# Spreading one number per token over the partitions: three bf16 parts on diagonals instead of fp32 products with the identity

## What is computed

```python
x = x + attention_windowed(_layernorm(x))     # 16 heads of 8, window +-16, token 0 global
x = x + ffn_ternary(_layernorm(x))
x = x + rglru(_layernorm(x))                  # gated linear recurrence, both directions
x = x + ffn_ternary(_layernorm(x))
x = x + attention_full_1(_layernorm(x))       # 16 heads of 8, softmax over 1024 tokens
x = x + moe(_layernorm(x))                    # top 1 of 8 experts, one shared We, capacity n // 8
x = x + attention_full_2(_layernorm(x))
x = x + moe(_layernorm(x))
```

```python
def _layernorm(x, axis=-1, eps=1e-05):
    m = jnp.mean(x, axis=axis, keepdims=True)
    v = jnp.var(x, axis=axis, keepdims=True)
    return (x - m) / jnp.sqrt(v + eps)
...
router_logits = h @ Wg
probs = jax.nn.softmax(router_logits, axis=1)
best = jnp.argmax(probs, axis=1)
mask = jax.nn.one_hot(best, E, dtype=probs.dtype)
gate = jnp.sum(probs * mask, axis=1)
...
out = combine.reshape(n, E * cap) @ expert_out     # = gate * (h @ We + be) for tokens within capacity
```

## Time and profile before

| | |
|---|---|
| median of 3 runs | 1068.19 us |
| lowest, highest | 1066.82, 1069.66 us |
| the profiled execution, its own time | 1069.15 us |
| its span in the profile | 1067.4 us |
| first full attention's loop starts at about | 345 us |
| last slot ends, run 4 alone from about | 1041 us |
| TensorE, VectorE, ScalarE, GpSimd busy | 91%, 78%, 68%, 16% |

### The profile page before, as it was taken

How to read it: one execution, slowest core, us unless ns; L and a number is a source line. 1 busy time by engine, 2 the same in 40 slices (tenths; PEclk the granted TensorE clock), 3 DMA queues, 4 the chain that set the end, 5 groups by cost and what they waited for, 6 DMA issues and landing times.

```text
span 1067.4 us, 32392 instructions
## 1 busy us (share of the span) xinstructions
PE 973.9 (91%) x13373; PEld 442.7 (41%) x13373; DVE 835.3 (78%) x1035; ACT 726.8 (68%) x1469; POOL 165.6 (16%) x438
## 2 busy tenths in 40 slices
PE   6799999779786999999999999999999999999997
PEld 2445545433342234344444444444434444433443
DVE  4545745164854999999999899999989998998923
ACT  3613544348332499999777789977779986797880
POOL 8200101016300000000011220011231001100100
PEclk8789989879877999999999999999999999999999
DMA  3763432200008213220000015410003530010000
GB/s 108 199 196 87 108 88 76 63 1 1 1 11 261 61 48 76 63 46 19 27 14 15 13 55 151 93 27 13 13 24 108 122 73 13 13 39 27 13 28 24
DMA packets 60386, 64.47 MB, mean 60 GB/s; under 512 B 17424, under 2 KB 39184, under 8 KB 60112
## 3 DMA queue, kind: packets, MB, share of 16 engines
q1 hardware_dynamic: 60240, 62.40, 22.0%
HBM read 27.06 MB, written 35.32 MB: 58 GB/s over the span
## 4 chain that ended last, share of the span: by engine, by line
DVE 56%; PE 32%; issue 5%; DMA 3%; ACT 3%; SPq 1%; POOLq 0%; POOL 0%; DVEq 0%; ACTq 0%
DVE nmf L1676 47%; PE wide L692 22%; PE bank L692 10%; DVE xcsq L1447 1%; DVE xp L1447 1%; DMA x<-xT 1%; ACT scr L1206 1%; DVE xcsq L1456 1%; SPq L447 1%; DMA KQs<-mw_dram 1%; DVE res L1447 1%; ACT L1206 1%; DVE nmt L1615 1%; DVE big L1830 1%; DVE big L1447 0%
## 5 line engine op out<-in xcount | busy, mean ns | idle before, releaser
L1676 DVE TENSOR_REDUCE nmf<-wide 128x1 f32<-128x1024 f32 x512 | 589.4, 1207 | 16.4 <-PE wide L692 15.6
L1206 ACT ACTIVATE big<-wide 128x512 f32<-128x512 f32 x683 | 391.3, 601 | 82.5 <-PE wide L692 70.9
L692 PE MATMUL wide<-big,KQs 48*128 48x512 bf16 (+1 forms) x1376 | 348.9, 343 | 3.8 <-DVE nmf L1676 2.1
L692 PE MATMUL bank<-big,V 128*9 128x128 f32 x8192 | 320.2, 274 | 11.9
L692 PEld LDWEIGHTS bank<-big,V 128*9 128x9 f32 x8192 | 177.3, 90 | 232.3 <-ACT big L1206 194.8
L692 PE MATMUL wide<-KQs,big 50*128 50x512 bf16 (+1 forms) x1035 | 266.4, 323 | 0.0
L1206 ACT ACTIVATE big<-bank 128x512 f32<-128x512 f32 (+1 forms) x469 | 231.6, 514 | 39.5 <-PE bank L692 33.7
L692 PE MATMUL bank<-KQs,big 50*128 50x512 bf16 x341 | 130.6, 383 | 0.0
L1206 ACT ACTIVATE scr<-wide 128x380 f32<-128x380 f32 (+3 forms) x128 | 61.3, 487 | 84.3 <-PE wide L692 73.4
L621 POOL CAST nms<-nmf 128x4 bf16<-128x4 f32 x128 | 24.0, 188 | 587.0 <-DVE nmf L1676 587.0
L692 PEld LDWEIGHTS wide<-KQs,big 50*128 50x128 bf16 x1035 | 69.8, 94 | 102.8 <-issue 51.7
(11 more groups left out here) (214 smaller groups left out, 785.3 us busy)
## 6 DMA issues: line engine op xcount, KB each, us to landing
o_dram<-big SPq DMA_DIRECT2D x128, 64.0 KB
big<-kf_dram SPq DMA_DIRECT2D x32, 200.0 KB
kf_dram<-scr SPq DMA_DIRECT2D x24, 256.0 KB, 3.4
qf_dram<-scr SPq DMA_DIRECT2D x24, 256.0 KB, 3.8
KQs<-qf_dram SPq DMA_DIRECT2D x32, 192.0 KB
ow_dram<-scr SPq DMA_DIRECT2D x32, 142.5 KB
big<-kw_dram SPq DMA_DIRECT2D x16, 275.0 KB
kw_dram<-scr SPq DMA_DIRECT2D x12, 352.0 KB, 5.7
```

What stands on the lines that cost most here:

```text
L692: return nc.tensor.matmul(o, l, r, start=start, stop=stop, **kw)
L1206: return nc.scalar.activation(o, i, f, **kw)
L1676: nc.vector.tensor_reduce(nmf[:, i % 4, c:c + 1], wide[:, k:k + 2, :].rearrange("p g c -> p (g c)"), AX.X, ALU.max, negate=True).then_inc( ...
```

## The change

Each number v of a spread is split by GpSimd into three bf16 parts whose sum is v: first = bf16(v), second = bf16(v - first), third = the rest. Tile t's part i goes to column 32 t' + (t' + 8 i) within a 128 x 256 bf16 array `parts`: the slices have step 33, so each part lies on a diagonal of 32x32 blocks, and what is between stays zero from a memset. One VectorE transposition (in 32x32 blocks, all of `parts[:, 0:32 * tiles]`) gives `rows`. TensorE then multiplies four times with a 0/1 matrix `quarter[:, g, :]`, whose partitions 32 g to 32 g + 31 are one: each product sums 32 partitions of `rows` in bf16, 32 * tiles columns wide, and gives the numbers of 32 tokens of every tile on all 128 partitions. The result stands in another order of columns (quarter, tile, token instead of tile, quarter, token), and VectorE's product reads it so, in pieces of 32 columns. The table `TICK` gets new steps and new places. One program of steps serves `norm1`, `norm2` and `gate`.

```diff
@@ -160,6 +160,9 @@
         rc = xcsq
 
         tall = scr[:, 5 * S:5 * S + 256].rearrange("p (t j) -> p t j", j=32)
+        parts = scr[:, 5 * S + 256:5 * S + 384].bitcast(BF16)
+        rows = scr[:, 5 * S + 384:5 * S + 512].bitcast(BF16)
+        quarter = scr[:, 5 * S + 512:5 * S + 768].bitcast(BF16).rearrange("p (g c) -> p g c", g=4)
         mgb = scr[:, 3072:3072 + S]
         lns = sb("lns", [P, 2, NT])
         me = sb("me", [P, NT, E])
@@ -221,7 +224,8 @@
         r_decay, r_in, r_square, r_root = sem("r_decay"), sem("r_in"), sem("r_square"), sem("r_root")
         r_drive, r_scan, r_sum = sem("r_drive"), sem("r_scan"), sem("r_sum")
         r_out_mm, r_y, r_gelu2, r_ld_mm = sem("r_out_mm"), sem("r_y"), sem("r_gelu2"), sem("r_ld_mm")
-        c_dve, c_square, c_rstd = sem("c_dve"), sem("c_square"), sem("c_rstd")
+        c_dve, c_square = sem("c_dve"), sem("c_square")
+        c_parts, c_turned = sem("c_parts"), sem("c_turned")
         c_exp, c_onehot, c_gate, c_x = sem("c_exp"), sem("c_onehot"), sem("c_gate"), sem("c_x")
         c_first, c_second, c_third = sem("c_first"), sem("c_second"), sem("c_third")
         x_out, stored = sem("x_out"), sem("stored")
@@ -297,10 +301,11 @@
 
         ORDER = [(d, c) for b in range(B) for d in range(2) for c in (2 * b, 2 * b + 1)]
 
-        TICK = {"sel": 0, "wo": 3, "mean1": 6, "square1": 8, "var1": 12, "rstd1": 13, "norm1": 15, "logits": 19,
-                "onehot": 21, "exp": 22, "we0": 22, "we1": 23, "total": 24, "count": 25, "gate": 30, "add": 33,
-                "mean2": 40, "square2": 42, "var2": 47, "rstd2": 48, "norm2": 51, "k0": 53, "part_k0": 55,
-                "k1": 56, "part_k1": 58, "q0": 59, "part_q0": 61, "q1": 62, "part_q1": 64, "v0": 63, "v1": 64}
+        TICK = {"sel": 0, "wo": 3, "mean1": 6, "square1": 8, "var1": 12, "rstd1": 13, "turn1": 15, "norm1": 17, "logits": 20,
+                "onehot": 22, "exp": 23, "we0": 23, "we1": 24, "total": 25, "count": 26, "split": 28, "turn": 30,
+                "gate": 32, "add": 35, "mean2": 39, "square2": 40, "var2": 44, "rstd2": 45, "turn2": 47, "norm2": 49,
+                "k0": 52, "part_k0": 54, "k1": 55, "part_k1": 57, "q0": 58, "part_q0": 60, "q1": 61, "part_q1": 63,
+                "v0": 62, "v1": 63}
         M_STEPS = ("sel", "wo", "mean1", "var1", "norm1", "logits", "count", "gate", "mean2", "var2", "norm2",
                    "k0", "k1", "q0", "q1")
         S_STEPS = ("we0", "we1", "v0", "v1")
@@ -336,9 +341,9 @@
                 if name in S_STEPS:
                     s_index[r, name] = len(s_index)
 
-        def norms(r, name):
-
-            return (2 * r if r < 2 else 2 + r) + int(name[-1]) - 1
+        def spreads(r, name):
+
+            return 3 * min(r, 2) + 2 * max(r - 2, 0) + {"norm1": 0, "gate": 1, "norm2": 2}[name]
 
         def squares(r, name):
 
@@ -647,10 +652,29 @@
                         g = rb[:, 0, 512 * n:512 * n + 512]
                         pool.tensor_tensor(g, g, rc[:, 512 * n:512 * n + 512], ALU.mult).then_inc(r_drive, 1)
 
+            pool.wait_ge(pv_evac, UNITS)
+            step(pool.memset(parts[:, :], 0.0))
+            step(pool.memset(quarter[:, :, :], 0.0))
+            for g in range(4):
+                step(pool.memset(quarter[32 * g:32 * g + 32, g, :], 1.0))
             for t in range(1, 5):
                 add_means(t)
                 if t == 2:
                     recurrent()
+
+            def split_parts(s, v, rest):
+                n = v.shape[1]
+                first, second, third = [parts[:, 8 * i:8 * i + 33 * (n - 1) + 1:33] for i in range(3)]
+                if s:
+                    pool.wait_ge(c_turned, s)
+                pool.wait_ge(c_parts, 5 * s + 1)
+                pool.tensor_copy(first, v).then_inc(c_parts, 1)
+                pool.wait_ge(c_parts, 5 * s + 2)
+                pool.tensor_tensor(rest, v, first, ALU.subtract).then_inc(c_parts, 1)
+                pool.wait_ge(c_parts, 5 * s + 3)
+                pool.tensor_copy(second, rest).then_inc(c_parts, 1)
+                pool.wait_ge(c_parts, 5 * s + 4)
+                pool.tensor_tensor(third, rest, second, ALU.subtract).then_inc(c_parts, 1)
 
             def chain(r, name):
                 if name in ("square1", "square2") and r != LAST:
@@ -660,7 +684,14 @@
                 if name in ("rstd1", "rstd2"):
                     ts = slice(4 * RUN_CHUNKS[r][0], 4 * RUN_CHUNKS[r][-1] + 4)
                     pool.wait_ge(mx_read, m_index[r, "var" + name[-1]] + 1)
-                    pool.tensor_tensor(lns[:, 1, ts], lns[:, 0, ts], power[:, ts], ALU.pow).then_inc(c_rstd, 1)
+                    v = lns[:, 1, ts]
+                    pool.tensor_tensor(v, lns[:, 0, ts], power[:, ts], ALU.pow).then_inc(c_parts, 1)
+                    split_parts(spreads(r, "norm" + name[-1]), v, lns[:, 0, ts])
+                if name == "split":
+                    ts = slice(4 * RUN_CHUNKS[r][0], 4 * RUN_CHUNKS[r][-1] + 4)
+                    pool.wait_ge(c_gate, r + 1)
+                    pool.tensor_copy(lns[:, 1, ts], mgate[:, ts]).then_inc(c_parts, 1)
+                    split_parts(spreads(r, "gate"), lns[:, 1, ts], lns[:, 0, ts])
                 if name == "add" and r != LAST:
                     pool.wait_ge(mx_read, m_index[r, "gate"] + 1)
                     for c in RUN_CHUNKS[r]:
@@ -1011,6 +1042,13 @@
 
                     return v[:, P * t0:P * (t0 + tiles)].rearrange("p (t g j) -> p t g j", g=4, j=32)[:, :, g, :]
 
+                def spread(k, tiles, s):
+                    pe.wait_ge(c_turned, s + 1)
+                    o = wide[:, k:k + 2, :].rearrange("p b c -> p (b c)")
+                    for g in range(4):
+                        ins = mm(o[:, 32 * tiles * g:32 * tiles * (g + 1)], quarter[:, g, :], rows[:, 0:32 * tiles])
+                    return ins
+
                 def fill(r, count):
 
                     if r == LAST:
@@ -1048,10 +1086,7 @@
                             ins = mm(wide[32 * g:32 * g + 32, k, 0:32 * tiles], meanw[:, 0:32], columns(sq, t0, tiles, g))
                     if name in ("norm1", "norm2"):
                         fill(r, FILL["norm1"])
-                        pe.wait_ge(c_rstd, norms(r, name) + 1)
-                        for t in range(tiles):
-                            ins = mm(wide[:, k + t // 4, P * (t % 4):P * (t % 4) + P],
-                                     lns[:, 1, t0 + t:t0 + t + 1].broadcast_to((P, P)), ident[:, :])
+                        ins = spread(k, tiles, spreads(r, name))
                     if name == "logits":
                         fill(r, FILL["logits"])
                         pe.wait_ge(mx_read, m_index[r, "norm1"] + 1)
@@ -1068,10 +1103,7 @@
                         ins = mm(wide[:, k + 1, 0:tiles * E], ones[:, :], hot)
                     if name == "gate":
                         fill(r, FILL["gate"])
-                        pe.wait_ge(c_gate, r + 1)
-                        for t in range(tiles):
-                            ins = mm(wide[:, k + t // 4, P * (t % 4):P * (t % 4) + P],
-                                     mgate[:, t0 + t:t0 + t + 1].broadcast_to((P, P)), ident[:, :])
+                        ins = spread(k, tiles, spreads(r, name))
                     if name in ("k0", "k1", "q0", "q1"):
                         pe.wait_ge(mx_read, m_index[r, "norm2"] + 1)
                         ins = mm(wide[:, k, :], w("w%s2" % name[0]), xn(2 * b + int(name[1])))
@@ -1694,6 +1726,17 @@
                         k = 2 * (n % 2)
                         both = wide[:, k:k + len(chunks), :].rearrange("p g c -> p (g c)")
 
+                    def by_group(v):
+                        return v.rearrange("p (t g j) -> p t g j", g=4, j=32)
+
+                    def grouped(v):
+                        return v.rearrange("p (g t j) -> p t g j", g=4, j=32)
+
+                    if name[0:4] == "turn":
+                        s = spreads(r, "norm" + name[4:] if name[4:] else "gate")
+                        dve.wait_ge(c_parts, 5 * s + 5)
+                        nc.vector.transpose(rows[:, 0:32 * tiles], parts[:, 0:32 * tiles]).then_inc(c_turned, 1)
+
                     def turned(n):
                         return tall[:, 0:n, :].rearrange("p t j -> p (t j)")
 
@@ -1722,7 +1765,8 @@
                         nc.vector.tensor_scalar(lns[:, 0, ts], tall[:, 0:tiles, 0], LN_EPS, None, ALU.add).then_inc(mx_read, 1)
                     if name in ("norm1", "norm2"):
                         at = HALF + P * (t0 % KT)
-                        tt(xp[:, b, at:at + P * tiles], xc[:, span], both, ALU.mult).then_inc(mx_read, 1)
+                        tt(by_group(xp[:, b, at:at + P * tiles]), by_group(xc[:, span]), grouped(both),
+                           ALU.mult).then_inc(mx_read, 1)
                     if name == "logits":
                         d(nc.vector.transpose(turned(tiles), wide[:, k, 0:32 * tiles]))
                         logits = tall[:, 0:tiles, 0:E]
```

(2 more changed lines are left out.)

## The result

Over five executions each, the changed kernel takes 1063.04 us in the median (1061.55 to 1064.36) and the kernel before 1067.43 (1066.44 to 1069.66). The ratio is 0.9944, with a 95% interval of 0.9928 to 0.9961: some 6 us less (4.2 to 7.7). A second set of seven executions on another chip gives 0.9933 (0.9907 to 0.9958). So the changed kernel is faster, by more than the 0.3% (3.2 us) that the prediction took as the least it could tell. The forecast was 2.5 us less, with "same" as the likeliest. The median lies 0.04 us above the lower end of the range, 1063.0, but that range was counted from 1068.19 for the kernel before. As a ratio its lower end is 0.9951, and the measured 0.9944 lies beyond it.

What follows compares the result with a forecast made beforehand. VectorE was taken to set the loop's pace at 4.57 us per slot. Loop -5.4, run 4 +2.0 and its clock +0.9 gave -2.5 us, a median from 1068.19 to 1065.7, range 1063.0 to 1069.8.

Steps and rivals of the forecast that it cites:

- What bounds the kernel: Attention loop: VectorE sets the pace at 4.57 us per slot; TensorE and ScalarE alone need 4.56.
- Waits removed in the loop: Eight spreads of 8 tiles lose 7.8 us of VectorE waiting, run 3 another 0.8: 8.6 us less.
- Transpositions: One more on VectorE per spread in the loop, eight at 0.35 and two at 0.22 us: 3.2 us more.
- GpSimd in the loop: The split's parts are ready 0.7 us ahead of the transposition at norm1; cost zero.
- Run 4: Longer chain at norm1 (+0.84 us) and gate (+1.1), together +2.0 us, ends 1.7 and 2.1.
- The clock in run 4: TensorE idling 2.2 us ahead of norm1 brings half clock; three groups at 0.3 us more each, +0.9.
- The product's new order: VectorE reading PSUM in pieces of 32 columns costs zero; upper end half pace, 1.07 us per 128 x 1024.
- Rival 3: Products of the spreads: short PSUM pieces halve VectorE's pace, 10.7 us, 1076.4; chance 0.10 shared with rival 4.
- rival 4: Split late in the loop if a strided GpSimd instruction takes over 0.45 us: 1076; chance 0.10 shared with Rival 3.
- Rival 2: TensorE and ScalarE's loop takes over; half of the 7.8 us returns as small waits: 1069.6; chance 0.11.
- The sum: Whole kernel: -5.4 + 2.0 + 0.9 = -2.5 us, profiled execution from 1069.15 to 1066.6.
- Rival 1: TensorE's clock holds in run 4: 3.4 us less, 1064.8; chance 0.27.

## Why the prediction was off

- **What bounds the kernel**: right. VectorE sets the loop's pace, TensorE and ScalarE follow. The doubled transposition cost its full 0.33 us, the doubled product a third of its 0.44.
- **Waits removed in the loop**: the mechanism was right, the term mis-sized. All eight brackets went, 7.8 us. But a spread is worth 0.81 to 0.84 us net (4.88 / 6, 5.04 / 6, and 1.64 / 2 in run 2), and the bracket less the transposition, 0.98 - 0.36, is only 0.62. The missing 0.2 lies around the bracket. Neighbours on VectorE overlap by 0.08: the product starts at 550.72, the maxima ahead of it end at 548.48 + 2.31 = 550.79. A wait breaks that overlap, so it costs its bracket and 0.08. Another part lies behind the stall: in the kernel before, the four maxima behind a product that had waited take 4.60 us, 1.15 each instead of 1.13, since the fourth starts 0.06 late, a wait too short for a bracket (timeline, VectorE, run 2):

```profile
904.38 1.22 DVE L1447 TENSOR_TENSOR xp<-xcsq,wide 128x1024 f32<-128x1024 f32 x1 [0.98 <-PE wide L692]
905.51 4.68 DVE L1676 TENSOR_REDUCE nmf<-wide 128x1 f32<-128x1024 f32 x4
910.11 0.44 DVE L1727 STREAM_TRANSPOSE scr<-wide 128x256 f32<-128x256 f32 x1
```

  Together these are 0.14 or so of the 0.2; the rest I can't place. Eight spreads make 8 x 0.2 = 1.6 us. In run 3 the wait of 0.44 behind the product of norm1 did not go but fell to 0.10 (from 987.17 to 987.27 us in the changed kernel). In its place one ahead of the product went, of 0.12 (993.01 to 993.13 before), and the overlap came back. The two spreads gave 0.80 net, where the sum had 0.8 - 0.44 = 0.36. Another 0.4.
- **What the prediction did not price**: the new places of k0 to v1. This is the step that failed most. The prediction priced what the spread needs (time for split and transposition) and put the new places of k0 to v1 at nothing, without a reason. They are worth 1.8 to 1.9 us, half of the error in the loop. In the trace of before the two waits that went could be read, 0.79 and 0.95 behind the reciprocals. The longer wait of 1.45 at k0, where the other three of its kind show 0.8, catches the eye first and was worth nothing: it moved to q1.
- **Transpositions**: right, 0.43 long, 0.36 from its start to the next instruction's (0.42 and 0.35 forecast).
- **GpSimd in the loop**: right in its zero; 0.51 to 0.58 us to spare at the norms instead of 0.7.
- **Run 4**: power to product 2.01 instead of 1.25 us, +0.76 (forecast +0.84); gate to product 2.26 instead of 1.25, +1.01 (+1.1). The links were 0.1 longer than taken, 1.57 and 1.82, the spread 0.2 shorter, 0.40 instead of 0.6: fp32 records were the wrong neighbour for a bf16 group. The estimate of 0.46 from the 81 ns of the Trainium skill ("TensorE: Matmul & The Clock Gate", "Back-to-back issue gap") was nearer, but the trace has less than 81 ns: with 0.22 us for one product, a group of 0.40 leaves 0.06 between two starts. Nor do four times 81 ns give 0.46; the prediction does not say what it added. Its upper end of +2.1 for run 4 doesn't follow from its terms either: with 0.61 for the spread they come to +2.0.
- **The clock in run 4**: +0.9 as a certainty was the wrong form. It was an event of three in eight, at 0.6 to 1.3 us each, and the profiled execution had none. The one case of half clock behind an idle stretch was read as a rule, and the earlier trace rows held a case against it: behind 2.95 us of idle time the group at 289.21 took 0.50 us, its length at 2.4 GHz, and the windows show a granted clock of 1.00 until 291.
- **The product's new order**: right, 1.20 us against 1.22. Rival 3 falls with it, and rival 4 with the 0.5 us that the split has to spare. Rival 2, the other loop, did not take back half of the 7.8, since a spread gave more than its bracket; with TensorE's products doubled it took back 0.15 us per spread.
- **The sum** for the profiled execution: -2.5 forecast; 1.6 more for the spreads, 0.4 in run 3, 1.8 for the places, 0.9 for the clock, 0.2 in run 4, and 0.6 ahead of the loop that can't be put down to the change: -8.0. The dips of the clock in run 3 add 0.2, and 0.3 stand behind the loop; that makes -7.5 against the -7.6 measured.

Nearly every term erred to the same side, so "same" came out likeliest where the changed kernel is faster by 0.56%. Rival 1 (the clock holds) had its term right for the profiled execution and, at 3.4 us less, was still 2.6 short of the 6 measured.

## What to carry to other kernels

Where an engine sets the pace, a removed wait is worth its bracket and what it broke around it, here 0.2 us on top of 0.9, of which 0.08 is the overlap with its neighbour. When a table of places changes, price every step that moved, not only those the change is about. Do it by the length of a stretch and not by one wait: 0.8 us less at k0 was 0.7 more at q1. And use a longer but lighter chain only where other work covers it: the new spread gained 0.81 to 0.84 us in the loop and cost 0.9 in run 4, and with the old one in run 4 that run is 1.77 us shorter.
